# One launch of a gated two-block transformer step: another order of the front, and part of its tail moved into the next pass

## The reference, cut to what matters

```
x: 16 sequences x 64 tokens x 256;  ctx: the same shape
x += tanh(g0) * self_attention(layernorm(x))                       # one head of 256
x += tanh(f0) * ternary_ffn(layernorm(x))   # weights rounded to -1,0,1; tokens and hidden rows to 8 bits; hidden 1024
y  = layernorm(x) * w + b
x += tanh(g1) * out_proj(fp8(cat(own, cross)))
     q, k, v = fp8(y / in_scale) @ wq, wk, wv    # 16 query heads, 8 key heads of 128; q and k normalised per head
     own     = grouped attention of q, k, v in a sequence
     qx      = fp8(y / in_scale) @ wqx ;  kx, vx = ctx @ w_kv_x ;  cross = grouped attention of qx, kx, vx
x += tanh(f1) * (shared expert + 3 of 7 routed experts)(x)
```

## Time and profile before

| | us |
|---|---|
| median of 3 runs | 690.55 (687.42 to 692.94) |
| the profiled execution, its own time | 688.03 |
| its span | 685.9 |
| TensorE busy | 594.1 (87% of the span) |
| VectorE, ScalarE, GpSimd busy | 499.8, 377.4, 367.2 |
| mean granted TensorE clock | 0.951 |

### The profile page before, as it was taken

How to read it: one execution, slowest core, us unless ns; L and a number is a source line. 1 busy time by engine, 2 the same in 40 slices (tenths; PEclk the granted TensorE clock), 3 DMA queues, 4 the chain that set the end, 5 groups by cost and what they waited for, 6 DMA issues and landing times.

```text
span 685.9 us, 10642 instructions
## 1 busy us (share of the span) xinstructions
PE 594.1 (87%) x3735; PEld 475.2 (69%) x3738; DVE 499.8 (73%) x951; ACT 377.4 (55%) x666; POOL 367.2 (54%) x299
## 2 busy tenths in 40 slices
PE   3795986589588999999999799999999989999995
PEld 1463332354266887788788688888888878888885
DVE  5589777689348999999996888988898765333332
ACT  1554758676268576666766655566666324533221
POOL 2320174200166877667866785666776732855421
PEclk9997998779789999999999999999999999999998
DMA  7950211003352103103147232112220100310001
GB/s 252 313 211 0 93 76 76 32 16 124 109 154 93 40 24 123 32 17 108 32 160 256 62 93 80 28 64 78 78 80 13 47 1 1 93 46 32 1 1 61
DMA packets 44563, 54.86 MB, mean 80 GB/s; under 512 B 8416, under 2 KB 30816, under 8 KB 44512
## 3 DMA queue, kind: packets, MB, share of 16 engines
q1 hardware_dynamic: 44512, 54.20, 23.8%
HBM read 41.60 MB, written 12.58 MB: 79 GB/s over the span
## 4 chain that ended last, share of the span: by engine, by line
PE 50%; DVE 10%; ACT 6%; issue 5%; POOL 2%; DMA 1%; DVEq 0%; POOLq 0%; ACTq 0%
PE g_proj L2049 9%; PE g_proj L2125 7%; PE g_scores L2083 6%; PE g_turn L2072 4%; PE g_op L2107 4%; DVE g_yb L1665 2%; PE g_op L472 2%; PE g_op L474 2%; PE g_op L473 2%; PE g_proj L457 2%; PE g_proj L459 2%; PE g_proj L458 2%; DVE g_ve L1626 2%; DVE g_qn L1639 1%; ACT g_qkT L1871 1%
## 5 line engine op out<-in xcount | busy, mean ns | idle before, releaser
L1519 POOL TENSOR_TENSOR g_rs<-g_ve,neg_half 128x4 f32<-128x4 f32 x80 | 85.3, 1072 | 65.3 <-DVE g_ve L1626 64.3
L2049 PE MATMUL g_proj<-w_hi,g_xqc 128*128 128x512 f32 x192 | 86.0, 448 | 9.1 <-POOL g_xqc L1513 6.0
L1843 ACT ACTIVATE g_sq<-g_proj 128x512 f32<-128x512 f32 x80 | 47.8, 598 | 60.7 <-PE g_proj L2049 59.7
L1535 POOL TENSOR_TENSOR g_cat<-g_yb,g_kb 128x1024 fp32r<-128x1024 bf16 x32 | 68.5, 2140 | 20.8 <-DVE g_yb L1681 20.8
L2049 PE MATMUL g_proj<-w_lo,g_xqc 128*128 128x512 f32 x192 | 78.8, 410 | 0.0
L1626 DVE TENSOR_REDUCE g_ve<-g_sq 128x4 f32<-128x516 f32 x80 | 54.8, 685 | 32.2 <-ACT g_sq L1843 31.6
L500 POOL TENSOR_TENSOR m_h_lo<-m_h,m_h_hi 128x512 fp32r<-128x512 f32 x32 | 41.3, 1294 | 58.6 <-ACT m_h_hi L487 58.6
L2072 PE MATMUL g_turn<-ident,g_qn 128*128 128x128 f32 x384 | 60.8, 283 | 11.0 <-ACT g_qkT L1871 5.1
L2072 PEld LDWEIGHTS g_turn<-ident,g_qn 128*128 128x128 f32 x384 | 45.0, 144 | 27.6 <-issue 6.9
L1276 PE MATMUL f_bank<-f_w_ctx,f_ctxT 128*128 128x512 f32 x128 | 60.2, 610 | 1.6 <-ACT f_kept L1064 1.4
L2083 PE MATMUL g_scores<-g_qkT 128*128 128x64 f32 x512 | 61.3, 273 | 0.0
(11 more groups left out here) (232 smaller groups left out, 1683.9 us busy)
## 6 DMA issues: line engine op xcount, KB each, us to landing
kvx_rows<-f_kept SPq DMA_DIRECT2D x32, 256.0 KB, 2.4
g_ksq<-kvx_rows SPq DMA_DIRECT2D x8, 512.0 KB, 4.6
g_kraw<-kvx_rows SPq DMA_DIRECT2D x16, 256.0 KB, 3.6
g_v<-kvx_rows SPq DMA_DIRECT2D x8, 512.0 KB, 4.8
m_raw<-in_L_W SPq DMA_DIRECT2D x16, 256.0 KB, 3.1
c_raw<-in_L_wqT SPq DMA_DIRECT2D x4, 512.0 KB, 8.3
f_w_ctx<-in_L_wkvxT SPq DMA_DIRECT2D x4, 512.0 KB, 7.8
x_raw<-in_L_wqxT SPq DMA_DIRECT2D x4, 512.0 KB, 3.8
```

Of the source, the lines that this page charges most:

```text
L1519: G.tensor_tensor(rs[:, at % 2, :], ve[:, at % 2, :], k["half"][:, 0:4], ALU.pow).then_inc(q["rs_done"], 1)
L1535: G.tensor_tensor(cat[:, h].rearrange("p h (b s) -> p b h s", b=2), yb[:, h, :].rearrange("p (b h s) -> p b h s", b=2, s=SEQ), kb[:, h, :] ...
L1843: A.activation(sq[:, at % 2, :, 0:D], bank(n, i)[:].rearrange("p (h d) -> p h d", d=D), ACT.Square, scale=D ** -0.5).then_inc(q["sq_done"], 1)
L2049: last = T.matmul(bank(n, i)[:], xqc[:, n % 2, view * KT + c_, :], w[:, c_, :], start=c_ == 0 and part == 0, stop=c_ == KT - 1 and part == 1)
```

## The change

No computation is added or dropped. Four things are moved:

- the rounding of the second group (units 8 to 15) goes out of the front: `over_scale` in the pass's lead-in, and on VectorE `late_tokens(view)`, five instructions of 1024 columns each, views 0 and 1 in the lead-in and views 2 and 3 at the head of own step 0;
- the low parts 6 and 7 of the weights are made in the lead-in;
- the eight products of context chunk 1 are made in the lead-in (in the two banks of `op`), and kept and stored there; `norm_keys(0)` and the loads of output weights 0 and 1 stand behind these stores on the SyncE queue;
- the orders of all engines are others, in the front, in the lead-in and in the own and cross steps; the output weights are split in the order 2, 3, 0, 1.

The core of the diff:

```diff
-        PRODUCTS = [(tile, chunk) for chunk in (2, 3, 0, 1) for tile in range(TILES)]
+        PRODUCTS = [(tile, chunk) for chunk in (2, 3, 0) for tile in range(TILES)]
 front, GpSimd
             weights.centre(pool, 4)
-            centre_context(0)
             ln.on_pool(pool, 3)
-            weights.centre(pool, 5)
-            centre_context(1)
-            (weigh(0, 0..3), rms(0), weigh(1, 0..3), rms(1))
+            weigh(0, 0..3); centre_context(0); weigh(1, 0); rms(0); weights.centre(pool, 5)
+            weigh(1, 1); centre_context(1); weigh(1, 2); weigh(1, 3); rms(1)
 front, VectorE, the last third
-            ... hidden_largest(1, 0); hidden_largest(1, 1); mean_square(1); hidden_largest(1, 2)
-            add_ffn(0); hidden_largest(1, 3); hidden_scales(1); ln.moments(4)
-            hidden_integer(1, 0); hidden_integer(1, 1); reciprocal; ln.apply(4)
-            hidden_integer(1, 2); hidden_integer(1, 3); low(3); low(4); round_two(0); add_ffn(1)
-            ln.moments(5); round_two(2); ln.apply(5); low(5); low(6); low(7); round_two(4, 6, ... 14)
+            ... hidden_largest(1, 2); hidden_integer(0, 2); hidden_largest(1, 3); hidden_integer(0, 3)
+            hidden_scales(1); low(5); hidden_integer(1, 0); add_ffn(0); ln.moments(4)
+            hidden_integer(1, 1); hidden_integer(1, 2); ln.apply(4); hidden_integer(1, 3)
+            round_two(0); add_ffn(1); ln.moments(5); round_two(2); ln.apply(5); round_two(4); round_two(6)
 front, ScalarE, the last third
-            keep_hidden(0, 0..3); keep_context(16); keep_context(17); high(5); high(6); high(7)
-            round_hidden(1, 0..3); weigh_tokens(0); (keep_hidden(1, j); over_scale(j)) x4 ...
+            keep_hidden(0, 0); keep_context(16); round_hidden(0, 2..3); keep_context(17); keep_hidden(0, 1)
+            keep_context(18); round_hidden(1, 0); keep_hidden(0, 2..3); round_hidden(1, 1) ...
 lead-in, SyncE
-                norm_keys(0)
-                for i in range(4):
-                    own_out.load(sp, t, i)
+                own_out.load(sp, t, 2)
+                own_out.load(sp, t, 3)
+                for e in range(TILES):
+                    sp.wait_ge(q["ctx_kept"], e + 1)
+                    sp.dma_start(k["kvx"][e, :, CH:2 * CH], late_kept[e % 4]).then_inc(stored[e % 4], 16)
+                own_out.load(sp, t, 0)
+                own_out.load(sp, t, 1)
+                for i in range(4):
+                    sp.wait_ge(stored[i], 32)
+                norm_keys(0)
 lead-in, TensorE (p: project, c: the moved products, t: turn)
-                p0 p1 t0 p2 p3 p4 t1 t2 p5 t3 p6 p7 t4
+                p0 p1 c0 t0 p2 c1 p3 t1 c2 p4 t2 c3 p5 p6 c4 p7 c5 t3 c6 c7 t4
 lead-in, VectorE
+                low(6); sums 0; ctx.mean(0); ... sums 3; late_tokens(0); sums 4; low(7) ... late_tokens(1); scale 5
 own step, ScalarE, step 0
-                own_out.high(2); key_squares; square(m, 0); exponent(n, 0); split_query(0); square(m, 1); scale(m, 0)
+                square(m, 0); square(m, 1); own_out.high(0); split_query(0); own_out.high(1)
+                exponent(n, 0); scale(m, 0); key_squares
 own step, VectorE
-                less_max 0; sums 0; total 0; less_max 1; sums 1; ctx.low or mean; scale 1 ... lift 0 ... lift 1
+                less_max 0; (step 0: late_tokens(2), late_tokens(3)); sums 0; sums 1; ctx.low or mean
+                total 0; less_max 1; scale 1 ... lift 0; lift 1       (lift 0 after unload, clip, power of half 1)
 own step, TensorE
-                turn(n, 5); scores(n, 0) ... turn(m, 0); project(m, 3) ... turn(m, 4); project(m, 7)
+                scores(n, 0); turn(n, 5) ... project(m, 3); turn(m, 0) ... project(m, 7); turn(m, 4)
 own step 0, GpSimd
-                low(2) after rstd(m, 0), low(3) at the step's end
+                low(0) first, low(1) after normalise(n, 0)
 cross step, ScalarE
-                ctx_out.high; key_squares; square(m, 2); exponent(n, 0) ... moe.keep; keep_pT(n, 1); scale(m, 3)
+                key_squares; exponent(n, 0); ctx_out.high; square(m, 2) ... keep_pT(n, 1); scale(m, 3); moe.keep
```

More of the change, by code:

```diff
@@ L195, in high, with low @@
         last.then_inc(self.hi_done, 1)
-    def low(self, dve, n):
-        dve.wait_ge(self.hi_done, n + 1)
+    def low(self, dve, n, earlier=False):
+        if not earlier:
+            dve.wait_ge(self.hi_done, n + 1)
         for c_ in range(KT):
@@ L998, in _ @@
             ln.apply(dve, 5, lambda j: qn[:, 1, j, :])
-            for n in range(5, 8):
-                weights.low(dve, n)
-            for u in range(4, UNITS, 2):
-                round_two(u)
+            round_two(4)
+            round_two(6)
         @block.scalar
@@ L1115, in _ @@
-            square(0, ST - 1)
-            for n in range(2 * ST):
-                gated(1, n)
-                keep_context(8 + n)
-                if n == 1:
-                    weights.high(act, 4)
-                if n % 2 == 1 and n > 1:
-                    square(1, n // 2 - 1)
-                if n > 3:
-                    round_hidden(0, n - 4)
+            gated(0, 0)
+            tern.scale(act, 2)
+            gated(0, 1)
+            gated(0, 2)
+            keep_context(3)
+            square(0, 0)
@@ L1125, in _ @@
+            square(1, 0)
+            keep_context(9)
+            gated(1, 3)
+            gated(1, 4)
+            gated(1, 5)
+            keep_context(10)
+            square(1, 1)
+            keep_context(11)
+            round_hidden(0, 0)
+            keep_context(12)
+            square(1, 2)
+            weights.high(act, 5)
+            gated(1, 6)
+            keep_context(13)
+            gated(1, 7)
+            round_hidden(0, 1)
+            keep_context(14)
             square(1, 3)
-            for j in range(ST):
-                keep_hidden(0, j)
+            keep_context(15)
@@ new lines, in _ @@
+            keep_context(19)
+            round_hidden(1, 2)
+            weights.high(act, 6)
+            keep_hidden(1, 0)
+            round_hidden(1, 3)
+            keep_hidden(1, 1)
+            keep_context(20)
+            weigh_tokens(0)
+            over_scale(0)
+            over_scale(1)
+            keep_hidden(1, 2)
+            over_scale(2)
+            over_scale(3)
+            keep_context(21)
+            keep_hidden(1, 3)
+            over_scale(4)
+            over_scale(5)
@@ L1149, in _ @@
+            over_scale(6)
+            weights.high(act, 7)
+            keep_context(22)
+            over_scale(7)
+            keep_context(23)
+            weigh_tokens(1)
         @block.tensor
@@ L1315, in _ @@
+            context(5)
+            gate_up(0, 6)
+            context(6)
+            turn_integers(1)
+            gate_up(0, 7)
+            gate_up(1, 0)
+            context(7)
+            gate_up(1, 1)
+            context(8)
+            gate_up(1, 2)
+            context(9)
+            gate_up(1, 3)
+            context(10)
+            gate_up(1, 4)
+            gate_up(1, 5)
+            context(11)
+            context(12)
+            context(13)
+            gate_up(1, 6)
             turn_hidden(0, 0)
-            for j in range(1, ST):
-                turn_hidden(0, j)
-                down(0, j - 1)
@@ L1573, in both @@
                         ctx_out.low(pool, 2 * (n - TILES + 1) + 1)
+                    if not cross(m):
+                        rstd(m, 3)
+                    if n in MATRIX:
+                        moe.low(pool, MATRIX[n])
                     normalise(n, 1)
@@ L1694, in ahead @@
                 def ahead(n):
+                    own.low(dve, 6, True)
                     dve.wait_ge(q["eps_made"], 1)
                     sums(n, 0)
+                    ctx.mean(dve, 0)
                     sums(n, 1)
```

567 lines of the change are left out of this document (338 added, 229 removed).

## The result

The changed kernel takes 664.16 us, the median of four runs (660.22 to 665.46), beside 691.60 for the kernel before (687.42 to 692.94, four runs). The ratio is 0.961, with a 95% interval of 0.956 to 0.966. The forecast was 669, in a range of 657 to 682.

What follows compares the result with a forecast made beforehand. A chain of waits, no full engine, bounds the front; TensorE nearly fills own and cross steps. Terms -19.0 - 10.5 + 12 + 0 - 2 - 2 = -21.5 from 688.03 give 666.5, 669 against the runs' median; range 657 to 682.

Steps and rivals of the forecast that it cites:

- the front's sum: Front up to the pass's release: the removed tail, -19.0 us, plus the new order of the front, -10.5.
- The tail: Front's end: products, keeps, rounding and low parts leave, so the release comes at 162.6 instead of 181.6, -19.0 us.
- The new order of the front: Front before its end: reordered lists remove waits behind spare work; -10.5 us, two thirds of -15.1, bounds 0 and -15.1.
- the layout by hand: Front's new lists laid out with profiled durations, every wait included but no semaphore latency or unforeseen queueing: -15.1 us.
- The lead-in: Lead-in and step 0: moved products, views and low parts plus a wait for own_out's load cost +12 us, bounds +8.3 and +17.
- The own steps: Seven own steps: no work changed, the 1.15 us wait for `normalise(n, 1)` mostly stays; 0, bounds -1 and +1 per step.
- Into cross attention: Step into cross attention: `exponent` no longer behind the high part waiting for its load, most of 1.76 us goes; -2 us.
- cross: Cross steps: `keep_pT(n, 1)` stands before the two copies of `moe.keep`, for which `attend` waits up to 1.30 us; -2 us.
- Rival C: Lead-in and step 0: VectorE's late views wait out GpSimd instructions, 4 to 5 us more, 674; chance 0.10.
- Rival A: Front: the layout holds in full, -15.1 instead of -10.5 us, 664; chance 0.15.
- Rival D: Own steps get longer, `lift(0)` waiting for the second half's `power`; at 4 us per step +28, 697; chance 0.05.
- Rivals B and E: B: front's new order brings nothing, 681, chance 0.13. E: B with Rival C or longer own steps, 685 to 690, 0.07.

Runs made afterwards that it cites:

- the two runs with 661.07 and 657.00 us: Changed kernel with late views 2 and 3 and a high part moved out of step 0, 661.07; that version with two low parts moved away from `p_lo`, 657.00.
- the first reordered version of the lead-in: Changed kernel with step 0 reordered: high parts and split behind exponent and scale(1, 0), sums ahead of late views 2 and 3, part 0 loaded early; 665.04 us.
- four experiments: Changed kernel with the own_out load early (665.73), second group's rounding back in the front (669.35), or step 0 reordered in two versions (665.04, 665.29).

## Why the prediction was right

Its sum was -21.5 against the profiled execution; measured were -27.8. Against the medians of the runs the miss is 4.8 us (669 forecast, 664.16 measured). The mechanism was right: the release comes earlier by the products and the rounding, and the lead-in pays part of it back. That the front's sum came out within 2 us (-29.5 forecast, -31.6 measured) is in part luck, since its two terms were wrong by 3.7 and 5.8 us in opposite directions.

- **The tail, -19.0: too large.** The tail alone is -15.3. The step's condition, that the four further products are covered by TensorE's idle time before 156.4, failed in the old order: they were reached only behind the last `down`, and ran 4.7 us past the point where the layer norm was ready. The step also left out low part 5, which stands ahead of the two pairs in the old order; VectorE's rounding ended 2.35 us later than the 161.1 of the sum.
- **The new order of the front, -10.5: too small.** It is -16.3 at the release, even more than the layout by hand (-15.1), in part because it alone makes room for those four products and takes low part 5 out of the way; these 3.7 us could be booked under the tail as well. In the medians it is -11.7; the profiled execution of the changed kernel is the fastest of its four, and what the others lose behind the release no profile shows. Both together: -31.6, forecast -29.5. The middle was laid out wrongly. `gate_up(0, 0)` starts at 62.4, not 65.6; the last `hidden` ends at 110.1, not at 105.9, so the FFN won 1.7 us and not 9. From there to the end of the rounding it is 38.7 us, near the 40.1 laid out. What lengthened the FFN in part is contention: VectorE has 44.27 us of busy time in it, and two low parts take 3.50 and 3.88 us beside `weigh` and `centre_context`, 1.41 elsewhere.
- **The lead-in, +12: right in size, wrong in one of its steps.** It is +12.7. The wait of `own_out.high(0)` for its load was forecast as seven microseconds on the path. The load was issued 30.9 us after the release (forecast 29.5) but landed in 4.2 us, not in 6.8 to 9.4; and ScalarE was busy with `over_scale`, keeps and squares until 0.1 us before. In the kernel before, all four loads were issued in a row behind the 512 KB that `norm_keys(0)` reads; here it had no other load ahead of it and one like it behind. With the load early nothing changed. `scores(0, 1)` ends 36.2 us after the release, 9.1 later than before, where 8 was forecast. That scale(1, 0) ended 42.9 us after the release, with 42.8 forecast, is luck, two errors that met: no wait for the load, but 1.38 us of waiting for GpSimd's `rstd`, behind VectorE's late views and `p_lo`.
- **The own steps, 0: too small.** They gave -3.5 in five in the trace; by the medians their order is worth nothing (663.84 with the old one). The step that the trace contradicts is "`normalise(n, 1)` comes no later, so the wait of 1.15 us stays in most part". That wait is gone, only with all four lists at once, and one of 0.70 us ahead of each output has come in its place.
- **Into cross attention, -2; cross, -2.** -2.7 and -1.7, and the run with the old order shows both to be of the order.
- **Rival C**, VectorE slowed by GpSimd, was real in a smaller size: two additions of 2.8 instead of 0.69 us and one mask of 0.93 instead of 0.43, 4.8 us of VectorE's time. What it is worth on the path, the two runs with 661.07 and 657.00 us show for their own order: 2.1 us at output(0). Rival A named the right direction of the front, with the wrong place. Rival D fell: the step became shorter, and moving `lift(0)` alone does nothing. Rivals B and E fell with the gain of the new order.

That the own steps' -3.5 does not show in the times is explained in part. In ten profiled executions with the new lists in the own steps (one of them with `lift(0)` moved), 7 of 50 steps between output(0) and output(5) took 23.4 us instead of 21.8; in four with an old list, none of 20 was lengthened so. The rows of one such step show the clock, and the step's start:

```profile
304.83:309.00 4.17, 4.17 (x22) 4.17 (x23) 2.61 (x5) 2.61 (x6) 4.17 (x4) 0.59 0.00 0
309.00:312.00 3.00, 3.00 (x20) 2.69 (x20) 1.56 (x3) 0.60 (x1) 0.59 (x1) 1.00 0.00 0
```

It is the first reordered version of the lead-in, from its output(4): a granted clock of 0.59 over the first 4.2 us, so mostly the lower level of 1.2 GHz. Ahead of it TensorE had waited 0.70 us for the second fp8, as it does ahead of every output in the new order. In each of the seven the clock is at its lower level for 3.4 us, from at most 0.6 us behind the output's start. Why these steps fall and the others don't stays open: the run with `lift(0)` moved, which waits 0.93 us for `less_max` there instead, had none in five steps, too few to tell. That these falls make up the whole difference between trace and medians is not shown.

## What to carry to other kernels

When two engines end at the same wait, taking one chain away leaves the wait where it is: four experiments left 6 to 9 us of gaps in step 0 before work itself was taken out of it. Look for the stretch in which the loaded engine is idle, not for a better order in the one where it is full. And when work of VectorE is moved into a stretch where GpSimd is busy, its kind counts: place reductions and work with its large input in PSUM beside GpSimd's long instructions, and not additions or scalings from SBUF to SBUF. And a time of one profile is compared only where the granted clock is the same in both: here a fall that came and went without an edit moved output(0) by 1.7 us.

## What the runs showed of the hardware

**The lock between VectorE and GpSimd.** `p_lo` takes 2.35 to 2.8 us on GpSimd. A VectorE instruction on two-byte data in SBUF, or with two inputs there, that starts while it runs ends about its own length behind it: 0.43 us became 2.49 (0.29 behind), 0.69 became 2.73, 2.81 and 2.84 (0.55 behind each). A scaling of fp32 in SBUF is held too, even one of four columns: in the changed kernel `f_xn` (128x256) took 2.45 instead of 0.35 us and `f_ms` (128x4) 2.34 instead of 0.16 beside a `weigh` in the front. Reductions (0.64) and a subtraction with one large input in PSUM (0.69) beside `p_lo` kept their length. It is waiting, not slower work. Not every instruction of GpSimd holds: beside `rstd`, which has four columns and takes 1.0 to 1.4 us, the two masks at 164.80 and 175.47 us started over 0.8 us ahead of its end and kept their 0.43. The Trainium skill states this as an exclusive lock of the shared port pair, held for a whole instruction ("SBUF — State Buffer", Who interferes with whom); the rows beside `p_lo` and `weigh` agree, those beside `rstd` do not show it.

**A shorter load.** The same load `c_praw` took 6.8 to 9.4 us in the kernel before and 4.2 to 5.3 in the changed one, where two of the four are issued behind the stores of the products. Their place in a row counts: two in a row landed 4.2 and 5.1 us (157.97, 158.45) and 4.2 and 5.3 us (181.11, 181.59) after their issue, three in a row (the early load) 4.2, 5.8 and 7.2. Before, four in a row behind the load of `norm_keys(0)` took 6.8, 7.7, 8.6 and 9.4.

**The clock.** The gap of 6.75 us in step 0 brings the granted clock to 0.50 from 190 to 195 us (1.2 GHz), and a 512-column matmul takes 0.63 instead of 0.40 us until about 198. Around 172 us gaps of 1.90, 2.15, 2.30 and 2.35 us were followed by a lower clock, those of 1.61, 2.08 and 2.18 us in other runs were not.
